# A convolution over channels on one NeuronCore: the column stage moved from 32x32 to 64x64 TensorE tiles, its matrices spread by VectorE

## What is computed

```python
y = x + (relu(nd[..., None] * W1[0] + b1) @ W2 + b2).transpose(2, 0, 1)[None]
ret = einsum('BGMTS,GMN->BGNTS', y, w + eye)
hq  = einsum('BGMTS,BTGIM->BGITS', y, qw1)
ret = ret + einsum('BGITS,BTGIM->BGMTS', hq, qw2)     # rank 2, one matrix per row T
hk  = einsum('BGMTS,BSGIM->BGITS', y, kw1)
ret = ret + einsum('BGITS,BSGIM->BGMTS', hk, kw2)     # rank 2, one matrix per column S
ret = ret + y * qdd (per row) + y * kdd (per column)
```

## Time and profile before

| | |
|---|---|
| three runs | 904.47, 905.84 and 910.92 us; median 905.84 |
| profiled execution | 898.13 us, its span 896.3 us |
| TensorE busy | 743.8 us, 83% of the span |
| GpSimd, VectorE, ScalarE busy | 57%, 50%, 43% |
| DMA | 149.12 MB, mean 166 GB/s |

### The profile page before, as it was taken

The page is one execution under the profiler, slowest core; times in us unless marked ns, Lnnn a source line. Parts: engine busy times, 40 slices in busy tenths (PEclk is TensorE's granted clock), DMA queues, the critical chain, the costliest instruction groups (busy, mean ns, idle before and its releaser), DMA issues. The chain is left out here.

```text
span 896.3 us, 31150 instructions
## 1 busy us (share of the span) xinstructions
PE 743.8 (83%) x14114; PEld 561.8 (63%) x14114; DVE 452.3 (50%) x484; ACT 388.4 (43%) x412; POOL 513.6 (57%) x459
## 2 busy tenths in 40 slices
PE   0567775899589975899879978899889978999894
PEld 0245554678478764677557755577657755678894
DVE  6597443377246723475336623466336624565253
ACT  3859523645365435533543334433543444332200
POOL 3536542277326831388559865698658955695042
PEclk9979888999989988999999988999999999999998
DMA  6776688838895989578983988469885978689169
GB/s 134 185 179 136 133 168 181 187 75 204 210 214 122 190 169 222 118 158 195 213 187 89 203 163 206 99 158 206 190 192 97 197 159 177 153 166 197 44 135 244
DMA packets 301024, 149.12 MB, mean 166 GB/s; under 512 B 30044, under 2 KB 296668, under 8 KB 300892
## 3 DMA queue, kind: packets, MB, share of 16 engines
q1 hardware_dynamic: 231456, 113.56, 58.3%
q10 hardware_dynamic: 69436, 33.58, 17.3%
HBM read 77.61 MB, written 69.47 MB: 164 GB/s over the span
## 5 line engine op out<-in xcount | busy, mean ns | idle before, releaser
L458 POOL TENSOR_TENSOR hidden<-log_table,row_scale 128x1024 f32<-128x1024 f32 x192 | 364.4, 1913 | 269.5 <-PE bias L768 261.4
L754 PE MATMUL main<-homes,mats_b 32*32 32x120 f32 (+1 forms) x9216 | 278.1, 270 | 95.5 <-issue 53.6
L754 PEld LDWEIGHTS main<-homes,mats_b 32*32 32x32 f32 x9216 | 252.2, 132 | 161.5 <-issue 102.8
L497 ACT ACTIVATE hidden<-hidden,b_col 128x1024 f32<-128x1024 f32 x192 | 220.8, 1151 | 286.0 <-POOL hidden L458 202.9
L743 PEld LDWEIGHTS main<-homes,mats_a 64*64 64x64 f32 x4096 | 257.3, 204 | 50.5 <-POOL mats_a L434 44.5
L665 DVE SCALAR_TENSOR_TENSOR homes<-bias,b_col,homes 64x512 f32<-64x512 f32 (+1 forms) x256 | 185.8, 747 | 183.1 <-DMA homes<-in_x 112.1
L743 PE MATMUL main<-homes,mats_a 64*64 64x128 f32 x4096 | 269.7, 286 | 0.0
L768 PE MATMUL bias<-hidden,w_blocks 128*64 128x512 f32 x768 | 205.8, 643 | 24.6 <-ACT hidden L497 14.4
L434 POOL TENSOR_TENSOR mats_a<-mats_in,own_block 128x256 f32<-128x256 f32 x256 | 150.6, 614 | 96.6 <-PE main L743 72.3
L647 DVE TENSOR_TENSOR homes<-main,homes 128x1024 f32<-128x1024 f32 x128 | 156.8, 1225 | 94.0 <-PE main L743 94.0
L637 DVE COPY homes<-main 128x960 f32<-128x960 f32 x64 | 74.1, 1157 | 147.9 <-PE main L754 147.7
(11 more groups left out here) (38 smaller groups left out, 32.4 us busy)
## 6 DMA issues: line engine op xcount, KB each, us to landing
homes<-in_x SPq DMA_DIRECT2D x200, 192.0 KB, 6.1
out_mixed<-homes ACTq DMA_DIRECT2D x104, 192.0 KB, 5.6
out_mixed<-homes SPq DMA_DIRECT2D x104, 192.0 KB, 5.5
homes<-in_x SPq DMA_DIRECT2D x72, 256.0 KB, 6.9
homes<-in_x SPq DMA_DIRECT2D x136, 64.0 KB, 4.9
mats_in<-a_mats SPq DMA_DIRECT2D x128, 64.0 KB, 4.1
out_mixed<-homes ACTq DMA_DIRECT2D x28, 256.0 KB
out_mixed<-homes SPq DMA_DIRECT2D x28, 256.0 KB
```

The costliest lines, as they stand in the source:

```text
L458: nc.gpsimd.tensor_tensor(hidden_tile(u, g).rearrange("p (j s) -> p j s", j=ROWS), bass.AP(logs.tensor, logs.offset, [list(logs.ap[0]), [1 ...
L497: nc.scalar.activation(hidden_tile(u, g), hidden_tile(u, g), ACT.Relu, bias=b1_col[:, 0:1])\
L754: mm = pe.matmul(main[of_group(g), i % 2, j * W:j * W + REGION_TILES[k] * ROWS], b_weights(g, C * ROWS + j), y_column(k, g, C * ROWS + j), ...
```

## The change

The group of partitions is now 64 wide with four blocks in it (`GS = 4`, two groups), for the column stage as for the row stage: partition = 64 q + 4 channel + block. A column step is then two 64x64 products per column instead of four of 32x32.

`mats_b` holds only the 16x16 matrices, 16 x 128 values per partition. A new VectorE instruction, `spread_columns`, multiplies 8 columns of it with the mask `own_block` and writes the block-diagonal matrices of one step into a ring of four (`spread_b`, 512 values per partition). Four of them run before region 0; then one at the beginning of every column step, three steps ahead. The ScalarE instruction that wrote zeros is gone, and the loads of `mats_b` are contiguous. TensorE waits for `columns_ready` at each column step.

Because the groups are wider, the row matrices come in two DMAs of 64 partitions in place of four of 32, and GpSimd spreads a unit in one instruction of 512 values in place of two of 256. x and the result use the same DMAs with another partition stride.

```diff
-GS = 2
+GS = 4
-QS = 4
-QUADS = BLOCKS // QS
-QP = H * QS
...
-A_UNIT = QP * UNIT
-HALVES = QS // GS
+A_UNIT = H * GS * UNIT
+B_RING = 4
+B_UNIT = H * GS * ROWS
...
-        mats_b = sb("mats_b", [P, GS * H * W])
+        mats_b = sb("mats_b", [P, H * W])
+        spread_b = sb("spread_b", [P, B_RING * B_UNIT])
...
-                    sp.dma_start(of_block(mats_b, GS * H * W, b, b % GS * W, [[GS * W, H], [1, W]]),
-                                 b_mats[b]).then_inc(b_in, DMA)
+                    sp.dma_start(of_block(mats_b, H * W, b, 0, [[W, H], [1, W]]), b_mats[b]).then_inc(b_in, DMA)
...
-                for part in range(HALVES):
-                    at = w % 2 * A_UNIT + part * GP * UNIT
-                    nc.gpsimd.tensor_tensor(
...
+                nc.gpsimd.tensor_tensor(
+                    mats_a[:, w % 2 * A_UNIT:(w % 2 + 1) * A_UNIT].rearrange("p (n b e) -> p n b e", n=H, b=GS),
+                    rows.unsqueeze(2).to_broadcast([P, H, GS, UNIT]),
+                    bass.AP(own_block, 0, [[GS, P], [0, H], [1, GS], [0, UNIT]]), ALU.mult).then_inc(unit_ready, 1)
...
-            nc.scalar.activation(mats_b[:], zero_col[:].to_broadcast([P, GS * H * W]), ACT.Copy)\
-                .then_inc(mats_zeroed, 1)
...
+            def spread_columns(e):
+                if e >= REGIONS * COL_TILES:
+                    return
+                if e >= B_RING:
+                    dve.wait_ge(main_ready, b_tile(*divmod(e - B_RING, COL_TILES)) + 1)
+                C = e % COL_TILES
+                dve.tensor_tensor(
+                    spread_b[:, e % B_RING * B_UNIT:(e % B_RING + 1) * B_UNIT].rearrange("p (n b j) -> p n b j", n=H, b=GS),
+                    mats_b.rearrange("p (n j) -> p n j", n=H)[:, :, C * ROWS:(C + 1) * ROWS].unsqueeze(2)
+                    .to_broadcast([P, H, GS, ROWS]),
+                    bass.AP(own_block, 0, [[GS, P], [0, H], [1, GS], [0, ROWS]]), ALU.mult).then_inc(columns_ready, 1)
...
             for T in range(REGION_TILES[0]):
                 add_bias(0, T)
+            dve.wait_ge(own_made, 1)
+            dve.wait_ge(b_in, PER_PIECE)
+            for e in range(B_RING):
+                spread_columns(e)
             compact("a")
             dve.wait_ge(logs_made, 4)
             for k in range(REGIONS):
                 for s in steps(k):
+                    if s < COL_TILES and k + s:
+                        spread_columns(k * COL_TILES + s + B_RING - 1)
                     if s >= COL_TILES:
                         finish_tile(k, s - COL_TILES)
...
             def b_columns(k, C):
                 i = b_tile(k, C)
+                e = k * COL_TILES + C
+                pe.wait_ge(columns_ready, e + 1)
                 taken, count = emptied(i - 2)
                 pe.wait_ge(taken, count)
                 for n in range(ROWS):
                     for g in range(GROUPS):
                         j = staggered(n, g)
                         mm = pe.matmul(main[of_group(g), i % 2, j * W:j * W + REGION_TILES[k] * ROWS],
-                                       b_weights(g, C * ROWS + j), y_column(k, g, C * ROWS + j), start=True, stop=True)
+                                       b_weights(g, e, j), y_column(k, g, C * ROWS + j), start=True, stop=True)
                 mm.then_inc(main_ready, 1)
```

More of the change, by code:

```diff
@@ L117, in build @@
         zeroed = sem("zeroed")
-        mats_zeroed = sem("mats_zeroed")
         own_made = sem("own_made")
@@ L139, in build @@
         b_in = sem("b_in")
+        columns_ready = sem("columns_ready")
         nd_ready = sem("nd_ready")
@@ L325, in load_mats_a @@
                 if v >= A_RING:
-                    sp.wait_ge(unit_ready, (v - A_RING + 1) * (CHUNK // UNIT) * HALVES)
+                    sp.wait_ge(unit_ready, (v - A_RING + 1) * (CHUNK // UNIT))
                 for g in range(GROUPS):
@@ L613, in _ @@
             dve.wait_ge(ident_made, 2)
-            step(dve.tensor_reduce(own_block[:], ident.rearrange("p (g m b) -> p g b m", b=GS, m=H),
-                                   mybir.AxisListType.X, ALU.add))
-            dve.tensor_tensor(own_block[:, 0:QS], own_block[:, 0:QS], own_block[:, QS:2 * QS], ALU.add).then_inc(own_made, 1)
+            dve.tensor_reduce(own_block[:], ident.rearrange("p (q b) -> p b q", b=GS), mybir.AxisListType.X, ALU.add)\
+               .then_inc(own_made, 1)
             dve.wait_ge(w2_in, DMA)
@@ L714, in staggered, with a_weights, b_weights, y_row @@
                 return (j + (ROWS // 2) * (g % 2)) % ROWS
-            def of_quad(q):
-                return slice(QP * q, QP * (q + 1))
-            def a_weights(q, w, row):
+            def a_weights(g, w, row):
                 pitch = 2 * A_UNIT
-                return bass.AP(mats_a, QP * q * pitch + w % 2 * A_UNIT + row, [[pitch, QP], [UNIT, QP]])
-            def b_weights(g, col):
-                return bass.AP(mats_b, GP * g * GP * W + col, [[GP * W, GP], [W, GP]])
-            def y_row(k, T, q, j):
+                return bass.AP(mats_a, GP * g * pitch + w % 2 * A_UNIT + row, [[pitch, GP], [UNIT, GP]])
+            def b_weights(g, e, j):
+                pitch = B_RING * B_UNIT
+                return bass.AP(spread_b, GP * g * pitch + e % B_RING * B_UNIT + j, [[pitch, GP], [ROWS, GP]])
+            def y_row(k, T, g, j):
                 at = y_slot(k, T) * COLS + j // 2 * 2 * W
-                return homes[of_quad(q), at:at + 2 * W].rearrange("p (s b) -> p s b", b=2)[:, :, j % 2]
+                return homes[of_group(g), at:at + 2 * W].rearrange("p (s b) -> p s b", b=2)[:, :, j % 2]
             def y_column(k, g, col):
@@ L736, in a_rows @@
                 w, part = divmod(tile_of(k, T), UNIT_TILES)
-                pe.wait_ge(unit_ready, (w + 1) * HALVES)
+                pe.wait_ge(unit_ready, w + 1)
                 taken, count = emptied(i - 2)
@@ L740, in a_rows @@
                 for n in range(ROWS):
-                    for q in range(QUADS):
-                        j = staggered(n, q)
-                        mm = pe.matmul(main[of_quad(q), i % 2, j * W:(j + 1) * W], a_weights(q, w, part * ROWS + j),
-                                       y_row(k, T, q, j), start=True, stop=True)
+                    for g in range(GROUPS):
+                        j = staggered(n, g)
+                        mm = pe.matmul(main[of_group(g), i % 2, j * W:(j + 1) * W], a_weights(g, w, part * ROWS + j),
+                                       y_row(k, T, g, j), start=True, stop=True)
                 mm.then_inc(main_ready, 1)
```

9 lines of the change are left out of this document (1 added, 8 removed).

## The result

| | before | after |
|---|---|---|
| timed runs beside each other | 904.47 to 910.92 us, median 907.87 | 871.76 to 873.30 us, median 872.56 |
| profiled execution, its span | 898.13, 896.3 us | 872.26, 870.5 us |

The ratio is 0.9612, 95% interval 0.957 to 0.9653: 3.9% faster, 35.3 us by the medians. The forecast was 883, so the sign and the range were right, and the gain was larger than the 23 us of the sum. The two profiled executions differ by only 25.9 us, because the one of before was faster than all timed runs beside it.

What follows compares the result with a forecast made beforehand. TensorE was taken as the busiest engine, held up by DMA of x before each landing and by late instruction packets behind it. Terms 9.9 + 6.9 + 10 + 2.4 - 1 - 5 = 23 us gave 875, plus 7.7 883 us; range 870 to 896.

Steps and rivals of the forecast that it cites:

- Two stretches and what sets each: Column stages: DMA sets row stage start to landing of x's second piece, TensorE sets landing to next row stage.
- Fewer instructions: Column steps: 32 records instead of 64, so packets keep up and all issue waits (53.6 us) go; 75 packets or so.
- The wider step: Column steps: a 64x64 step with 120 values takes 1.96 us (bounds 1.745 and 2.065), 0.215 us more than before.
- Region 0: Before row stage 0: four spreads and added DVE work, partly offset by fewer DMA issues; loss 1 us, bounds 0 and 6.
- Landing to row stage, regions 1 to 3: From landing of x's second piece to the next row stage: 29.2 us each, 87.7 against 97.6; gain 9.9 us.
- Regions 4 to 7, and GpSimd against VectorE: Landing to row stage 32.5 us each, gain 6.9; spreads waiting for GpSimd, 0.3 us per pair in 16 pairs, loss 5.
- the release of step 7: Regions 4 to 7: VectorE's add_bias, two spreads and copy after the landing, 1.41 + 1.24 + 1.15 = 3.8 us.
- "slower" rival: Column stages 4 to 7: spreads waiting for GpSimd make VectorE the pace, deciding from 1.6 us per spread; 916 us, chance 0.10.
- Row stage to landing: Before x's second piece lands: fewer row-matrix DMA issues on SyncE save 1.5 us in each of seven regions; gain 10, bounds 0 and 35.
- Column stage 8: Last column stage, no bias and no x: 33.11 us becomes 30.7; gain 2.4 us, bounds 0 and 4.
- From the sum to the median: The profiled 898.13 us less 23 gives 875; 7.7 us added because the median lay above that execution: 883.
- The signs that were named: Right: pairs about 3.9 us, issue waits under 10 us, late stretch 32.5; wrong: landings beyond 69.2 us, pairs near 4.2.

Runs made afterwards that it cites:

- e11: Changed kernel with column products on tiles of 64 rows and 32 columns, half of the column sums left out: 848.12 us in one run.
- e2: Changed kernel with only the first four spreads, so later column steps multiply with wrong matrices: 854.89 us.
- e4: Changed kernel with both spreads moved ahead of add_bias on VectorE: 866.98 us.
- e9: The kernel of e4 run once more beside the changed kernel, no further edit: 869.84 us, against 874.94 for the changed kernel.
- e3: Changed kernel with each load of row matrices as four DMAs of 32 partitions again: 883.97 us, against 872.56.
- e5: The kernel of e4 with ScalarE issuing six of a piece's eight stores instead of four: 871.53 us.
- e1: Kernel before, with the column stage multiplying only two of its four 32x32 groups, half of the column sums left out: 941.42 us.

## Why the prediction was right, and where its terms were off

**Two stretches and what sets each.** Right, and it carried all that followed: no row stage has a gap, and the changes fall in the column stages, before or behind the landing. "Nothing in it waits long for the later pieces" was not so for VectorE, which in the kernel before waited for a later piece for 4.5 to 5.1 us in regions 4, 6 and 7; but TensorE was held up behind it for 0.9 us at most.

**Fewer instructions.** Right: the issue waits are gone and 76 packets were moved, 75 foretold. e11 puts it at 17.6 us in regions 1 to 3.

**The wider step.** Wrong in size: the upper bound of 2.065 us was true, and 1.96 was taken, near what scaling with the values gives. Early pairs are 4.12 us, not 3.92. Ten steps of seven regions cost 7 us more than booked. Region 0 was hit hardest: with 64 values a step went from 1.05 to 2.0 us, 15 us in 16 steps, for which the sum had no term. The kernel before also had issue waits of 9.0 us there, which the sum did not count either; the longest is

```profile
96.74 0.86 PE L754 MATMUL main<-homes,mats_b 32*32 32x64 f32 x21 [5.63 <-issue]
```

Row stage 0 began at 102.8 instead of 97.5, a loss of 5.3 where 1 was booked, within its bounds of 0 and 6. e2, with the same wide steps and no later spreads, begins it at 99.6, so the steps and the first four spreads account for about 2.1 of these 5.3, and the later spreads for about 3.2, of which TensorE waited 2.66 in one place (83.75). Two runs of one kernel can differ by 1.4 here (e4 and e9).

**Landing to row stage, regions 1 to 3.** Foretold gain 9.9, measured 9.0 (29.4 to 29.8 each, 29.2 foretold).

**Regions 4 to 7, and GpSimd against VectorE.** The mechanism was right, its size was not. A gain of 6.9 less 5 was booked; it was a loss of 3.8. The step that failed is the release of step 7: the spreads between landing and copy were priced as undisturbed, with the copy's end 3.8 us after the landing, and it came at 5.0, 6.2, 6.7 and 3.7. The four stretches took 140.7 us where 130 was foretold: 6.4 of the difference are these copies, and 3.6 the wider step (nine steps of 0.1 us in each). The 5 us booked for the pairs behind were not lost there, since a pair took no longer than TensorE's own 5.99. That release had been priced as if GpSimd were idle, without a reason; in region 6 it began its hidden tiles 0.9 us after the landing. The "slower" rival was half true: the mean spread with its wait is 1.12 us, not 0.62, under the 1.6 at which it would decide, but two spreads of a late pair take 3.35, which is 1.68 each. It did not tip over, because with a pair of 5.99 us the point lies at 1.7.

**Row stage to landing.** Foretold 10 us in seven regions, measured 18.9 in regions 2 to 7. In region 1 another 5.0 came off, but row stage 0 had begun 5.3 later, so that this landing itself hardly moved (153.34 to 153.67). This term was the largest miss within the sum: 1.5 us a region was a guess between 0 and 5, and e3 measured 2.0. e3 gives 13.6 of the 18.9 us to the two DMAs; the other 5.3 are about what two runs of the same kernel differ by (420.6 and 425.7), and were not separated.

**Column stage 8.** 31.85 us, a gain of 1.3 where 2.4 was foretold; the wider step again.

**From the sum to the median.** The profiled executions differ by 25.9 us, near the 23 foretold, but that is luck: the stretch before the landing brought 13.9 us more than booked, and the other terms together 12.0 less (regions 4 to 7 5.7, region 0 4.3, column stage 8 1.1, regions 1 to 3 0.9). The rest of the miss is one step at the end: 7.7 us were added because the median before lay so much above the profiled execution. The changed kernel has no such distance, 872.26 in the profile and 872.56 in the median. The kernel before varies by 28 us from run to run, the changed one by 5. Issue waits that depend on when packets come would explain it, but e4 and e5, in whose traces no column product has one either, vary by 12 us; what makes runs vary stays open.

**The signs that were named.** Of those for right, the issue waits, the packets, the early stretch and the spreads (0.68 us alone, up to 2.4) came true, and no landing was later than 65.1 us after its row stage. The late stretch (33.9 to 36.9 us, not 32.5) and the pairs (4.12, not 3.9) did not, and three signs of being wrong appeared: pairs near 4.2, VectorE above 5.8 us a pair, and TensorE waiting for L636, though for 5.5 us in all and only in region 0. The time was right while these details were not.

## What to carry to other kernels

When TensorE waits "for issue" at regular counts of instructions, compare what it consumes per microsecond with what comes: fewer and larger products can win even if each costs more, as here in regions 1 to 3. Price a product on another tile shape from a row of that shape, and do not scale it with the values: here the 64 columns of the tile set its time. When work is added to an engine, look for what it can be made to wait for (an instruction of GpSimd, a late DMA ahead of it in the queue) and place it where neither is near.

## What had not been expected of the hardware

- A 32-bit product on a 64x64 tile took 124 to 129 ns per record for anything from 60 to 128 values; on a tile of 64 rows and 32 columns 109 ns with 120 values (3.49 us for 32 records per group), as on a 32x32 one, and 72 ns with 64 values (1.15 us for 16 records).
- In e1, with two 32x32 products side by side, the granted clock, once down to 1.2 GHz in a wait, stayed there in region 2 for the 33.8 us of uninterrupted products that were left until the row stage. In the kernel before, with four, the 128 records after the wait took 5.98 us and the next two steps 3.5 again; in the changed kernel the first 64 took 5.8 and the next 64 4.12.
- A VectorE instruction with two SBUF inputs took 0.68 us alone and up to 2.4 us beside a GpSimd one of 1.9; GpSimd's two tiles in turn took 4.2 us instead of 3.8.
